# Cross-attention packing split over two queues, tree weights loaded one by one, batch 0's tail one step earlier, maxima products spaced, a block of key products moved on GpSimd

## The reference

```python
x = x + attn_block(layernorm(x))                       # causal self-attention, an 8-step recurrence, a 1024-wide GELU layer
x = x + cross_attention(layernorm(x), ctx, ctx, ...)   # 16 heads of 16, context of 77 rows
x = x + tree_ffn(layernorm(x))                         # 8 trees of depth 7, 255 nodes each
```

## Time and profile before

| | |
|---|---|
| median of 3 runs | 1053.12 us (1051.53 to 1055.05) |
| profiled execution, its own time | 1051.39 us |
| its span, first to last instruction | 1049.7 us |
| PE busy | 911.2 us, 87% |
| DVE busy | 601.7 us, 57% |
| ACT busy | 471.6 us, 45% |
| POOL busy | 199.4 us, 19% |
| mean granted share of PE's clock | 0.92 |

### The profile page before, as it was taken

The page is one execution under the profiler, slowest core; times in us unless marked ns, Lnnn a source line. Parts: engine busy times, 40 slices in busy tenths (PEclk is TensorE's granted clock), DMA queues, the critical chain, the costliest instruction groups (busy, mean ns, idle before and its releaser), DMA issues. The chain is left out here.

```text
span 1049.7 us, 11784 instructions
## 1 busy us (share of the span) xinstructions
PE 911.2 (87%) x3897; PEld 555.6 (53%) x3912; DVE 601.7 (57%) x898; ACT 471.6 (45%) x681; POOL 199.4 (19%) x238
## 2 busy tenths in 40 slices
PE   5776689999999976999997799978596898889997
PEld 3553255555555423544445577744234666667775
DVE  4635767777777316377785754554345555446554
ACT  2311056565666743666654355525443323434332
POOL 7920012211222211000015500002227600000000
PEclk9897789999999997999998899996866998889999
DMA  3056534423343116000000000213744000000000
GB/s 123 11 200 170 216 95 111 102 72 91 94 123 98 36 53 235 3 0 0 1 1 18 1 1 7 49 37 67 161 115 122 22 1 20 1 1 21 1 21 20
DMA packets 27953, 66.15 MB, mean 63 GB/s; under 512 B 6048, under 2 KB 8992, under 8 KB 27520
## 3 DMA queue, kind: packets, MB, share of 16 engines
q1 hardware_dynamic: 23872, 59.90, 19.6%
q0 software_dynamic: 2496, 4.47, 2.2%
q10 hardware_dynamic: 1536, 1.14, 0.4%
HBM read 37.09 MB, written 19.14 MB: 54 GB/s over the span
## 5 line engine op out<-in xcount | busy, mean ns | idle before, releaser
L1193 DVE TENSOR_REDUCE part_max<-psum 128x4 f32<-128x512 f32 x288 | 185.9, 687 | 78.2 <-PE psum L1644 46.2
L863 ACT ACTIVATE prob<-psum 128x1024 f32<-128x1024 f32 (+1 forms) x192 | 145.3, 809 | 91.6 <-PE psum L1672 90.9
L1644 PE MATMUL psum<-k,q 128*128 128x512 f32 x288 | 121.9, 467 | 21.6 <-DMA k<-k 16.8
L1672 PE MATMUL psum<-q,k 128*128 128x512 f32 (+3 forms) x384 | 96.9, 358 | 10.8 <-ACTq L850 9.8
L724 POOL TENSOR_SCALAR_AFFINE_SELECT prob<-prob 128x256 f32<-128x256 f32 x128 | 52.6, 420 | 238.2 <-ACT prob L863 237.2
L1644 PEld LDWEIGHTS psum<-k,q 128*128 128x128 f32 x288 | 52.8, 196 | 85.1 <-DVE part_max L1193 54.2
L1046 ACT ACTIVATE silu<-psum,wt_bias 128x512 f32<-128x512 f32 x64 | 40.5, 684 | 120.2 <-PE psum L350 111.8
L1690 PE MATMUL psum<-prob,vq 128*32 128x512 f32 (+3 forms) x768 | 81.8, 498 | 2.1 <-POOL prob L724 1.2
L1672 PEld LDWEIGHTS psum<-q,k 128*128 128x128 f32 x384 | 66.2, 191 | 32.0 <-ACT prob L863 11.4
L1520 DVE TENSOR_TENSOR masked_lo<-masked,masked_hi 128x1024 fp32r<-128x1024 f32 x32 | 41.6, 1300 | 40.8 <-ACT masked_hi L1053 40.8
L348 PE MATMUL psum<-masked_hi,wt_hi 128*128 128x512 f32 x128 | 56.8, 443 | 4.0 <-DVE masked_lo L1520 4.0
(11 more groups left out here) (157 smaller groups left out, 1647.5 us busy)
## 6 DMA issues: line engine op xcount, KB each, us to landing
q<-q SPq DMA_DIRECT2D x8, 768.0 KB, 6.2
k<-k SPq DMA_DIRECT2D x16, 384.0 KB, 8.0
xq<-xq_b SPq DMA_DIRECT2D x36, 128.0 KB
q<-part_hi SPq DMA_DIRECT2D x16, 256.0 KB
k<-part_hi SPq DMA_DIRECT2D x16, 256.0 KB
o<-stage SPq DMA_DIRECT2D x8, 512.0 KB, 7.1
wt<-in_wt SPq DMA_DIRECT2D x8, 512.0 KB, 4.2
nrm<-in_xT SPq DMA_DIRECT2D x4, 512.0 KB, 5.3
```

Source lines behind the costliest of these rows:

```text
L863: act.activation(A.prob[0:A.keys, s % 2, p, :, q0:CH], psum[0:A.keys, 2 * p:2 * p + 2, q0:CH], ACT.Exp, scale=SCALE)\
L1193: dve.tensor_reduce(part_max[:].rearrange("q (j p i) k -> q p j i k", j=2, p=2)[:, :, :, i, kt], heads, AX_X, ALU.max).then_inc(A.s1_free, 1)
L1644: mm = pe.matmul(heads, A.q1[:, qd, i * P:(i + 1) * P], A.k1[:, qd, :, k0:k0 + P], start=True, stop=not diag)
L1672: mm = pe.matmul(psum[0:A.keys, 2 * p + j, q0:CH], A.k2[:, qd, p, j, kt * P:kt * P + A.keys], A.q2[:, qd, p, c * CH + q0:(c + 1) * CH], st ...
```

## The change

Five edits. (1) The sums stay on POOL (`pack_sums`, semaphore `xsum_in`), the values go to SP (`pack_values`, `xnum_in`), behind the next quad's queries; `invert_cross` waits for sums alone, `cross_out` and `normalize_cross` for both kinds. (2) The tree tiles 0 to 3 are issued one at a time, later; POOL splits them at other places. (3) Batch 0's normalising, projection and last norm move from steps 12 to 15 (and behind) to steps 11 to 15; `square(ln5)(1)` stands ahead of the last exponentials and `deviation(ln5)(0)` ahead of the last copy. (4) The third `cross_unit` of a step stands alone ahead of `cross_weigh`'s place, the fourth behind all that the step does beside; DVE's fourth maximum stands behind its other work of the step. At the start the third chunk's query projection stands ahead of the wait for `ff2`'s last sum. (5) On POOL the key products move behind the last two chunks' additions.

```diff
             load_neg(0)
-            load_neg(1)
-            for n in range(2, XQUADS):
-                b, m, qd = cross(n)
-                sp.wait_ge(xq_free, 2 * (2 * b + 1) + m + 1)
...
-                load_q(n, slice(0, SEQ))
+            for n in range(XQUADS):
+                if n + 1 < XQUADS:
+                    load_neg(n + 1)
+                if n + 2 < XQUADS:
+                    b, m, qd = cross(n + 2)
+                    sp.wait_ge(xq_free, 2 * (2 * b + 1) + m + 1)
...
+                    load_q(n + 2, slice(0, SEQ))
+                if n >= 1:
+                    pack_values(n - 1)
                 if n == 5:
                     sp.wait_ge(xq2_in[0], q_loaded(3))
-                    sp.wait_ge(xmx_ps, slot_of(3, 7) + 1)
                     load_tree(0)
+                if n == 6:
                     load_tree(1)
-                load_neg(n)
-            sp.wait_ge(xq2_in[1], q_loaded(7))
-            for t in (2, 3):
-                load_tree(t)
+                if n == 7:
+                    sp.wait_ge(xq2_in[1], q_loaded(7))
+                    load_tree(2)
+            pack_values(XQUADS - 1)
+            load_tree(3)
             sp.wait_ge(xpv_ps, 2 * XQUADS)
...
-                if c == 1:
-                    pool.wait_ge(xk_hi_s, KT)
...
+            pool.wait_ge(xk_hi_s, KT)
+            pool.wait_ge(c_ps, UNITS)
+            for h in range(P // HD):
...
-            for n in range(XQUADS):
-                pack_cross(n)
+            for n in range(4):
+                pack_sums(n)
                 if n % 2 == 1:
                     spread_cross(n // 2)
-                if n in (5, 6):
-                    for t in ((0, 1) if n == 5 else (2, 3)):
-                        split_weights(t)
+            pack_sums(4)
+            pack_sums(5)
+            split_weights(0)
+            spread_cross(2)
+            pack_sums(6)
+            split_weights(1)
+            pack_sums(7)
+            for t in (2, 3):
+                split_weights(t)
+            spread_cross(3)
             for t in range(4, TREES):
                 split_weights(t)
...
                 if n >= 2 and g % 2 == 0:
-                    act.wait_ge(xpack_in[n % 2], 16 * 5 * (n // 2))
+                    act.wait_ge(xnum_in[n % 2], 16 * 4 * (n // 2))
+                    act.wait_ge(xsum_in[n % 2], 16 * (n // 2))
...
-                if g == 14:
-                    square(ln5)(0)
+                if g in (13, 14):
+                    square(ln5)(g - 13)
+            deviation(ln5)(0)
             cross_out(2 * XQUADS - 1)
-            square(ln5)(1)
-            deviation(ln5)(0)
             deviation(ln5)(1)
...
                 for qd in range(2):
-                    dve.wait_ge(xpack_in[qd], 16 * 5 * (i + 1))
+                    dve.wait_ge(xsum_in[qd], 16 * (i + 1))
...
-                    for i in range(4 * s, 4 * s + 4):
+                    for i in range(4 * s, 4 * s + 3):
                         cross_max(n + 2, i)
...
+                if n + 2 < XQUADS:
+                    cross_max(n + 2, 4 * s + 3)
                 if g in (6, 9, 14):
                     invert_cross({6: 0, 9: 1, 14: 2}[g])
-                if g == 12:
+                if g == 11:
                     normalize_cross(0)
                     add_cross(0, 0)
...
-            pe.wait_ge(res4, 2 * NCH + 2)
+            xq_projection(2, 0)
             cross_turn(1)
-            xq_projection(2, 0)
...
                 cross_scores(g, 0)
+                if g == 0:
+                    pe.wait_ge(res4, 2 * NCH + 2)
...
                     cross_unit(n + 2, 4 * s + 1)
-                    cross_unit(n + 2, 4 * s + 2)
                 if g > 0:
                     cross_weigh(g - 1)
                 if n + 2 < XQUADS:
-                    cross_unit(n + 2, 4 * s + 3)
+                    cross_unit(n + 2, 4 * s + 2)
...
+                if n + 2 < XQUADS:
+                    cross_unit(n + 2, 4 * s + 3)
-                if g == 12:
+                if g == 11:
                     pe.wait_ge(xq_free, 8)
                     cross_project(0, 0)
```

More of the change, by code:

```diff
@@ L251, in layer @@
         xq2_in = [sem(f"xq2_in{i}") for i in range(3)]
-        xpack_in = [sem(f"xpack_in{i}") for i in range(2)]
+        xnum_in, xsum_in = [[sem(f"{n}{i}") for i in range(2)] for n in ("xnum_in", "xsum_in")]
         xrec, xrec_st, xden_in = sem("xrec"), sem("xrec_st"), sem("xden_in")
@@ L771, in pack_cross @@
-            def pack_cross(n):
+            pool.wait_ge(xk_hi_s, KT)
+            pool.wait_ge(c_ps, UNITS)
+            for h in range(P // HD):
+                ins = pool.tensor_scalar(kbd[:, h, :].rearrange("p (k n) -> p k n", k=KT), xk_hi, v_("hmask", h),
+                                         None, ALU.mult)
+            ins.then_inc(zeros_set, 1)
+            pool.wait_ge(xk_in, 16 * 12)
+            pool.wait_ge(zeros_set, 6)
+            for j in range(2):
+                ins = pool.tensor_scalar(xk2[0:XROWS + 2, j].rearrange("p m s n -> p (m s) n"),
+                                         xk_raw[0:XROWS + 2].rearrange("p m s n -> p (m s) n"),
+                                         v_("jmask", j, XROWS + 2), None, ALU.mult)
@@ L773, in pack_cross, with pack_sums @@
+            ins.then_inc(xkeys, 1)
+            pool.wait_ge(xkeys, 2)
+            def pack_sums(n):
                 b, m, qd = cross(n)
-                done = xpack_in[n % 2]
                 pool.wait_ge(xo_done, 2 * n + 2)
-                pool.dma_start(xsums[64 * qd:64 * qd + 64, 2 * b + m, :], stage[HD:P:32, qd, :]).then_inc(done, 16)
-                for h in range(4):
-                    pool.dma_start(quot_b[b][64 * qd + HD * h:64 * qd + HD * h + HD, 0, m, :],
-                                   stage[32 * h:32 * h + HD, qd, :]).then_inc(done, 16)
+                pool.dma_start(xsums[64 * qd:64 * qd + 64, 2 * b + m, :], stage[HD:P:32, qd, :]).then_inc(xsum_in[qd], 16)
@@ L1445, in normalize_cross @@
                 dve.wait_ge(xden_in, 16 * KT * (c // 2 + 1))
+                for qd in range(2):
+                    dve.wait_ge(xnum_in[qd], 16 * 4 * 2 * (c // 2 + 1))
                 num, den = [quot_b[c // 2][:, i, :, c % 2 * CH:(c % 2 + 1) * CH] for i in range(2)]
@@ L1970, in _ @@
                     mean(ln5)(1)
+                if g == 15:
+                    variance(ln5)(1)
             cross_weigh(2 * XQUADS - 1)
             spread_out(ln5)(0)
-            variance(ln5)(1)
             spread_out(ln5)(1)
```

44 lines of the change are left out of this document (19 added, 25 removed).

## The result

The changed kernel takes 1046.01 us (median of 14 runs, 1044.42 to 1051.06), the kernel before 1051.53 us (14 runs beside it, 1046.97 to 1060.17). The ratio is 0.9947, 95% interval 0.9927 to 0.9968: 5.5 us less, with 3.4 to 7.7 us inside the interval. The forecast was 8.3 us less. The direction was right and the size half too large. Taken one by one, the steps were wrong in more places than the sum shows.

The account below looks back on a forecast made before the run. PE has most work, so only its waits can be won, chiefly 8.26 us behind a reciprocal held by a shared semaphore. Terms -8.4 + 1.9 + 0 - 1.8 = -8.3 us, from 1053.12 to 1044.8; range 1040.5 to 1052.0.

Parts of the forecast that it names:

- Start projection and spacing: Cross-attention steps up to 9: start projection fills a 2.14 us wait, -1.5, spacing takes it back; together 0.
- Rival C: Behind the stall PE keeps 2.4 GHz instead of half clock, about 4 us more gained: 1040.8; chance 0.12.
- Second reciprocal: DVE in the cross-attention: waiting for sums alone, it is done at 752.6 instead of 761.23, 8.6 us earlier.
- batch 0's projection: `cross_project(0,0)` on PE in the cross-attention starts at 766.0 instead of 774.38: -8.4 us.
- the edit's gain is in the semaphore: Within the same full DMA engines sums land early (5.9 us at most), so splitting the semaphore wins, not bandwidth.
- the forecast's 4.4: Landing of the last quad's sums in the cross-attention: issued at 747.58, taken as landed at 752.0.
- Rival D: Nothing gained: the reciprocal stays at 760 because sums queue behind a broadcast on POOL, 1053; chance 0.10.
- 1.3 for contention: Extra us for the second broadcast sharing DMA engines with values and queries, added between reciprocal and batch 0's projection.
- The rest costs nothing: Later tree-tile splits are hidden by the tail, and SP's extra DMA issues stand where SP would wait: 0.
- rival E: Slower: values late on SP hold ACT's copies at steps 10, 12 and 14, +4.7 us, 1057.8; chance 0.08.
- Tail moved up: Batch 0's tail in the cross-attention: +3.85 for step 12, -3.45 before the first `spread_out`, +1.5 second variance: +1.9 us.
- Key products: Wide layer: PE's 3.62 us wait goes, 1.8 is given back by a sum meeting POOL's products: net -1.8 us.

Follow-up runs that it names:

- the data edits with the start projection: Changed kernel with the spacing and the move of batch 0's tail undone, leaving DMA edits, key products and start projection; ratio 0.9856 to the kernel before.
- the same with the tail up: Changed kernel with only the spacing of the maxima products undone, batch 0's tail still at its earlier steps; ratio 0.9891 to the kernel before.

## Why the prediction was right and wrong

*Start projection and spacing, 0 (bounds -2.1 and +2.2): the step that failed.* The two were to cancel. Start: -2.2, just past its bound; the wait of 2.14 us is gone whole. Spacing: +7.1 beside the other edits. The working looked at one turn, step 6, and put it 2.2 us later. Against the kernel without the spacing it was 5.7 us later, as the turns of steps 2 and 4 waited too and a longer stretch ran at half clock; at step 10 it was 11.5. "Step 9 then ends when it did, and the sums' landing sets the reciprocal" is the sentence that did not hold: the sums of quad 3 were issued 5.8 us later than before (753.36 for 747.58), and everything behind them hangs on that. Rival C had the clock on the wrong side. It asked whether it would stay at 2.4 GHz behind the stall; it fell ahead of it.

*Second reciprocal, -8.6 us, and batch 0's projection, -8.4 us: right in size without the spacing, by luck as to the reading; lost in the kernel with it.* The reading of the landings was wrong. "Their landing: 753.5 as a late bound; 747.58 + 2.1, the fastest sums, = 749.7 as the early one": both came from a shared semaphore, and with the semaphore alone split the sums landed 13.4 us after issue and nothing was won. So "the edit's gain is in the semaphore" was wrong. With values on SP, the tree tiles later and the start projection moved, but no spacing, the reciprocal and the projection came where the forecast had them (55.82 for 55.62, 69.51 for 69.57). That is two errors that cancel: the sums were issued 3.1 us earlier (1.6 of them by the start projection), where none was forecast, and needed 7.7 us to land for the forecast's 4.4. In after the spacing took it back, 63.62 and 76.26. There the sums of quad 2, issued 0.6 us behind the broadcast, landed with it; those of quad 3, issued 7.1 us behind it, took 6.7 us:

```profile
quot_b<-xr POOLq DMA_DIRECT2D x1, 512.0 KB, 7.6
xsums<-stage POOLq DMA_DIRECT2D x1, 16.0 KB, 7.3
```

From the end of the reciprocal to the projection after took 772.74 − 760.65 = 12.1 us; the forecast's 12.1 was exact and its 1.3 for contention not needed.

Rival D, given 0.10, had the reciprocal right, at 760, and part of the reason: sums behind a broadcast do land late, but in after they were above all issued late. Its consequence, no gain at all, didn't come.

*Behind the projection: 3.7 us that the sum doesn't have.* It passed the 8.4 us on to the end in full. With spacing and tail undone the projection came 8.4 us earlier than before and the first logits only 4.8. PE's wait ahead of the second `spread_out` was 2.65 us in the four kernels with the old order of DMAs and splits and 3.8 to 4.4 in the nine with the new one. "The rest costs nothing" is therefore short by some 1.2 to 1.7 us. A likely part is POOL's later tree split, which the first chunk's `nrm_lo` meets: in after it took 1.79 us from 804.39, beginning inside the split (802.75 + 2.35), against 1.23 before, and it stands ahead of the inverse that PE waited 4.38 us for. No run moves the splits alone. No copy of ACT waited for `quot_b<-stage`, so rival E is out.

*Tail moved up, +1.9: wrong sign, -3.2 to -3.3.* The sum charged 3.85 us of step 12 and credited 3.45. It left out that the first variance's wait shrinks too, 3.12 to 0.66 us, and put 1.5 for the second's, which was 1.53. Waits alone would have made the move worth nothing (10.19 against 10.12 us); the gain came from less half clock, which no term held. It isn't a property of the move: with the sums on ACT it lost 1.0 us.

*Key products, -1.8: mechanism right, give-back too large.* -3.0 by two pairs of kernels, inside the bounds. `total_squares` of chunk 2 took 0.68 us:

```profile
583.61 0.68 DVE L1112 TENSOR_TENSOR wide<-wide 128x512 f32<-128x512 f32 x1
...
607.50 1.22 DVE L1095 TENSOR_TENSOR wide<-res 128x512 f32<-128x512 f32 x1
608.64 4.20 DVE L1311 SCALAR_TENSOR_TENSOR nrm_lo<-nrm,vec,nrm_hi 128x512 fp32r<-128x512 f32 x2
```

The sum met the first `xk2` product (605.13 us, half of 6.90) and took 1.22 us instead of 0.69, not the 1.5 to 4 forecast; PE's wait for it rose from 0.79 to 1.29. What was held for 4.20 us is `third_low`, for which PE didn't wait. On POOL the products were quicker than in the old place (8.77 us for eight, 6.90 for two, against 11.24 and 7.42), and ended at 612.0.

Now the sum. Before, the data edits with the start projection, the same with the tail up, and after form a chain, and their stages give −4.8 − 3.3 + 7.1 us for the cross-attention and −3.6 for the wide layer, together −4.6. This is the difference of the two profiles, divided among the edits, and no check on it; the 5.5 us measured are the check. Part by part, measured for forecast: spacing +7.1 for +1.5, data edits −3.2 for −8.4, tail −3.3 for +1.9, start −2.2 for −1.5, key products −3.0 for −1.8. Two parts came out over 5 us worse and one 5 us better, so that −8.3 came as near to −4.6 as it did is in good part luck. How the 3.2 us of the data edits divide between values on SP and later tree tiles was not separated.

## What to carry to other kernels

A landing time is only worth what its semaphore can tell apart: where several DMAs raise one, give each kind its own in a trial run before the time of one goes into a sum. A small DMA issued behind a large one landed with it or later here, whichever of three engines issued it, so put the small ones ahead, all of them, also the next link of the chain. An edit that is put at zero needs its own run as much as one that is put at eight: here the spacing ate what the others had won. And compare two executions from an event that both have, not by their clocks: here the kernel that reached the wide layer 12 us late was 7 us quicker from the first turn on.

## What the runs showed of the hardware that was not expected

16 KB of sums took 3.0 us ahead of a 512 KB broadcast and 7.3 to 13.6 us just behind one from POOL's queue; from ACT's they took up to 10.1 us while one was in flight. PE's clock fell at 740 us in after, behind a wait of 1.90 us; the same wait at the same place left it full for another 16 to 17 us in two other spaced kernels (741 to 757 and 758). Two of DVE's two-operand sums in SBUF that met a product on POOL ended about 0.15 us behind it: one took 3.45 us against 0.68 for the same sum alone, the other 1.22 against 0.69. The Trainium skill, "SBUF — State Buffer", section "SBUF: two separate sides", tells of a port pair that DVE and GpSimd lock for a whole instruction; these rows agree.
